# Median and 1x1 mix of a wavelet convolution block: the other term of images 1, 4, 8 and 11 added by TensorE with a unit matrix in place of POOL's five sums

## What is computed

```python
def _L0_conv_ref(x, ...):          # wavelet branches, 3x3 convolution, batch norm with ReLU
    y = lax.conv_general_dilated(rimg, convW_w, window_strides=(1, 1), padding='SAME', ...)
    y = y + convW_b[None, :, None, None]
    return batchnorm_relu(y, bnW_gamma, bnW_beta)

def _L1_conv_ref(x, W, b):
    x_denoised = median_blur(x, KSIZE)                   # 3x3 median of each channel
    y = jnp.einsum('bchw,oc->bohw', x_denoised, W) + b[None, :, None, None]
    return x + y
```

## Time and profile before

| | us |
|---|---|
| median of three runs | 402.18 (400.51, 402.18, 403.07) |
| the profiled execution, its own time | 403.58 |
| its span, first to last instruction | 401.2 |
| busy in the span: PE / PEld / DVE / ACT / POOL | 383.8 / 205.1 / 372.2 / 170.8 / 232.5 |
| mean granted TensorE clock, share of full speed | 0.991 |

### The profile page before, as it was taken

The page is one execution under the profiler, slowest core; times in us unless marked ns, Lnnn a source line. Parts: engine busy times, 40 slices in busy tenths (PEclk is TensorE's granted clock), DMA queues, the critical chain, the costliest instruction groups (busy, mean ns, idle before and its releaser), DMA issues.

```text
span 401.2 us, 3603 instructions
## 1 busy us (share of the span) xinstructions
PE 383.8 (96%) x1106; PEld 205.1 (51%) x1106; DVE 372.2 (93%) x487; ACT 170.8 (43%) x351; POOL 232.5 (58%) x213
## 2 busy tenths in 40 slices
PE   6889999999999999999999999999999999998776
PEld 2245578866454555555555545454545464443222
DVE  2889967999999999999999999999999999999994
ACT  2456674446252433333334343333424221379661
POOL 3999559460694664738474747465564740016791
PEclk9999999999999999999999999999999999999988
DMA  7980010010101001010101010101011000002665
GB/s 290 418 364 2 2 52 2 0 52 2 53 1 52 17 37 52 0 52 0 54 0 52 1 54 1 52 1 52 8 46 33 19 2 1 0 0 119 247 248 223
DMA packets 7793, 26.69 MB, mean 67 GB/s; under 512 B 992, under 2 KB 1248, under 8 KB 7776
## 3 DMA queue, kind: packets, MB, share of 16 engines
q1 hardware_dynamic: 7776, 26.48, 17.6%
HBM read 18.09 MB, written 8.39 MB: 66 GB/s over the span
## 4 chain that ended last, share of the span: by engine, by line
PE 81%; DVE 12%; POOL 3%; DMA 2%; issue 1%; SPq 0%; ACT 0%; DVEq 0%
PE conv_ps L429 60%; PE conv_ps L444 12%; PE one_ps L411 4%; PE one_ps L530 3%; DVE y L1004 2%; PE conv_ps L554 2%; DMA z<-x 2%; POOL y L241 1%; POOL y L242 1%; DVE one_ps L916 1%; DVE one_ps L925 1%; DVE sorted_cols L876 1%; DVE sorted_cols L923 1%; DVE one_ps L910 1%; DVE sorted_cols L883 1%
## 5 line engine op out<-in xcount | busy, mean ns | idle before, releaser
L429 PE MATMUL conv_ps<-ru,wt 128*128 128x512 f32 (+1 forms) x324 | 129.9, 537 | 0.0
L429 PEld LDWEIGHTS conv_ps<-ru,wt 128*128 128x128 f32 x324 | 61.3, 190 | 55.1 <-issue 52.7
L429 PE MATMUL conv_ps<-xu,wt 128*128 128x496 f32 (+3 forms) x216 | 86.6, 537 | 0.0
L663 ACT ACTIVATE y<-conv_ps,sgn 128x512 f32<-128x512 f32 (+1 forms) x36 | 24.4, 679 | 124.1 <-PE conv_ps L429 124.1
L429 PEld LDWEIGHTS conv_ps<-xu,wt 128*128 128x128 f32 x216 | 41.0, 190 | 35.6 <-issue 33.7
L248 POOL TENSOR_TENSOR ru<-z 128x512 f32<-128x512 f32 x14 | 18.2, 1301 | 59.3 <-DVE one_ps L916 59.3
L342 POOL TENSOR_TENSOR ru<-eo 128x512 f32<-128x512 f32 x16 | 17.0, 1062 | 47.5 <-DVE one_ps L874 47.4
L429 PE MATMUL conv_ps<-ru,v 128*128 128x496 f32 (+3 forms) x108 | 43.3, 537 | 0.0
L554 PE MATMUL conv_ps<-z,w 128*128 128x512 f32 x64 | 32.7, 653 | 7.4 <-POOL z L387 4.1
L411 PE MATMUL one_ps<-y,w 128*128 128x512 f32 x64 | 30.5, 601 | 5.1 <-POOL y L242 1.8
L620 ACT ACTIVATE z<-z,bn 128x256 f32<-128x256 f32 x64 | 33.1, 595 | 0.4 <-DVE bn L819 0.4
(11 more groups left out here) (141 smaller groups left out, 741.1 us busy)
## 6 DMA issues: line engine op xcount, KB each, us to landing
z<-x SPq DMA_DIRECT2D x16, 512.0 KB, 10.5
raw_place<-x SPq DMA_DIRECT2D x15, 512.0 KB, 3.2
out<-y SPq DMA_DIRECT2D x15, 512.0 KB, 2.6
wt<-w_t SPq DMA_DIRECT2D x2, 576.0 KB, 10.8
ru<-x SPq DMA_DIRECT2D x1, 512.0 KB, 14.1
out<-y SPq DMA_DIRECT2D x2, 256.0 KB, 2.6
w<-w_t SPq DMA_DIRECT2D x2, 64.0 KB, 7.9
vec<-vectors SPq DMA_DIRECT2D x1, 3.0 KB, 8.3
```

Source lines behind the costliest of these rows:

```text
L429: return nc.tensor.matmul(bank(u, b)[:, (r0 - row) * BW:(r1 - row) * BW], taps(half, kx, ky), plane[:, (r0 + dy) * BW:(r1 + dy) * BW], sta ...
L663: S.activation(at(slot(n), row * W + b, [[2, cols]]), src, ACT.Identity, scale=sgn[:, :], accum_out=y_sum[:, part:part + 1]).then_inc(y_ke ...
```

## The change

Images 1, 4, 8 and 11 (`SUMMED`, four in place of five) get their other term on TensorE. POOL's map makes max(scale3 * y, -shift3) for them, which is ReLU(scale3 * y + shift3) without the shift; behind each of the two products with w2 TensorE multiplies this by a unit matrix into the same bank, so that PSUM holds the sum; ScalarE copies it out to y with the bias shift3 + cb2, and from there it is sent. ScalarE's norm of y (line 720) and POOL's sums (lines 393 and 398) go. The other twelve images are finished as before, by VectorE: images 3, 7, 9 and 12 are new among them, images 4, 8 and 11 have left. The unit matrix is made by POOL (a memset and an affine_select of 128 x 128) in the tensor of w1, which is no longer needed then, once POOL's part in the convolution is done. One column, neg_shift3, is added to the second batch norm. The mix of image 15 goes to `one_ps`, where its own median had its rows, and doesn't wait for image 13 to be read out of `conv_ps`.

```diff
-    SUMMED = (1, 3, 7, 9, 12)
+    SUMMED = (1, 4, 8, 11)
...
+        unit = w1
...
                 if n in SUMMED:
-                    sp.wait_ge(out_by_pool, SUMMED.index(n) + 1)
+                    sp.wait_ge(out_by_act, SUMMED.index(n) + 1)
...
+            G.memset(unit[:, :], 1.0).then_inc(ones_set, 1)
+            pool.wait_ge(ones_set, 1)
+            G.affine_select(out=unit[:, :], in_=unit[:, :], pattern=[[-1, CH]], base=0, channel_multiplier=1,
+                            compare_op=ALU.is_equal, fill=0.0).then_inc(unit_made, 1)
+
             def map_x1(n):
-                G.tensor_scalar(slot(n), slot(n), scale3[:, :], shift3_bias2[:, :], ALU.mult, ALU.add).then_inc(x1_by_pool, 1)
+
+                if n in SUMMED:
+                    G.tensor_scalar(slot(n), slot(n), scale3[:, :], neg_shift3[:, :], ALU.mult, ALU.max).then_inc(x1_by_pool, 1)
+                else:
+                    G.tensor_scalar(slot(n), slot(n), scale3[:, :], shift3_bias2[:, :], ALU.mult, ALU.add).then_inc(x1_by_pool, 1)
...
-                if n in OWN:
-                    map_x1(n)
-                if n - 3 in SUMMED:
-                    pool.wait_ge(x1_by_act, SUMMED.index(n - 3) + 1)
-                    pool.wait_ge(mix_kept, SUMMED.index(n - 3) + 1)
-                    G.tensor_tensor(slot(n - 3), slot(n - 3), zslot(n - 3), ALU.add).then_inc(out_by_pool, 1)
+                map_x1(n)
             map_x1(IMAGES - 1)
...
-            def mix(n, k):
+            def mixed(n):
+
+                return one_ps[:, 0, :] if n == IMAGES - 1 else conv_ps[:, n % 2, :]
+
+            def mix(n):
...
-                    mm = nc.tensor.matmul(conv_ps[:, k, half], w2[:, :], zslot(n)[:, half], start=True, stop=True)
+                    mm = nc.tensor.matmul(mixed(n)[:, half], w2[:, :], zslot(n)[:, half], start=True, stop=n in OWN)
+                    if n in SUMMED:
+                        pe.wait_ge(x1_by_pool, n + 1)
+                        mm = nc.tensor.matmul(mixed(n)[:, half], unit[:, :], slot(n)[:, half], start=False, stop=True)
...
-            for n in range(2, IMAGES):
+            for n in range(2, IMAGES - 1):
                 if n - 2 in SUMMED:
-                    pe.wait_ge(mix_kept, SUMMED.index(n - 2) + 1)
+                    pe.wait_ge(out_by_act, SUMMED.index(n - 2) + 1)
                 else:
                     pe.wait_ge(out_ready, OWN.index(n - 2) + 1)
-                mix(n, n % 2)
+                mix(n)
+            mix(IMAGES - 1)
...
                 norm_median(n)
-                if n in SUMMED:
-                    S.activation(slot(n), slot(n), ACT.Relu, bias=shift3[:, :], scale=scale3[:, :]).then_inc(x1_by_act, 1)
                 if n - 2 in SUMMED:
                     act.wait_ge(mix_done, n - 1)
-                    S.activation(zslot(n - 2), conv_ps[:, n % 2, :], ACT.Identity, bias=cb2).then_inc(mix_kept, 1)
+                    S.activation(slot(n - 2), conv_ps[:, n % 2, :], ACT.Identity, bias=shift3_bias2[:, :]).then_inc(out_by_act, 1)
...
+                after(1)
+                step(V.scalar_tensor_tensor(neg_shift3[:, :], mid3[:, :], scale3[:, :], b3, ALU.mult, ALU.subtract))
                 V.scalar_tensor_tensor(shift3_bias2[:, :], mid3[:, :], neg_scale3[:, :], beta_bias2[:, :], ALU.mult, ALU.add).then_inc(bn3_ready, 1)
...
-                dve.wait_ge(x1_by_pool, OWN.index(n) + 1)
+                dve.wait_ge(x1_by_pool, n + 1)
```

More of the change, by code:

```diff
@@ L124, in wavelet_conv_median_kernel @@
         zero_cols = at(zeros[:, :], 0, [[0, BANK // CH], [1, CH]])
-        singles = sb("singles", [CH, 19])
+        singles = sb("singles", [CH, 20])
         (abs_g3, neg_abs_g3, signed_b, beta_bias2, y_total, sq_total, mean3, off3, neg_off3, sq_eps3, var3, sd3, r3, newton3,
-         scale3, neg_scale3, shift3, shift3_bias2, mid3) = (singles[:, k:k + 1] for k in range(19))
+         scale3, neg_scale3, shift3, shift3_bias2, mid3, neg_shift3) = (singles[:, k:k + 1] for k in range(20))
         conv_ps = ctx.enter_context(nc.psum_tensor("conv_ps", [CH, 2, PIX], fp32))
@@ L189, in wavelet_conv_median_kernel @@
         med_normed = sem("med_normed")
-        x1_by_act = sem("x1_by_act")
         x1_by_pool = sem("x1_by_pool")
@@ L194, in wavelet_conv_median_kernel @@
         mix_done = sem("mix_done")
-        mix_kept = sem("mix_kept")
-        out_by_pool = sem("out_by_pool")
+        ones_set = sem("ones_set")
+        unit_made = sem("unit_made")
+        out_by_act = sem("out_by_act")
         out_ready = sem("out_ready")
@@ L562, in _ @@
             pe.wait_ge(w2_in, 16)
+            pe.wait_ge(unit_made, 1)
             pe.wait_ge(squares_summed, PARTS_ALL)
             for n in range(2):
-                mix(n, n)
-            for n in range(2, IMAGES):
+                mix(n)
+            for n in range(2, IMAGES - 1):
                 if n - 2 in SUMMED:
-                    pe.wait_ge(mix_kept, SUMMED.index(n - 2) + 1)
+                    pe.wait_ge(out_by_act, SUMMED.index(n - 2) + 1)
                 else:
                     pe.wait_ge(out_ready, OWN.index(n - 2) + 1)
-                mix(n, n % 2)
+                mix(n)
+            mix(IMAGES - 1)
         @block.scalar
@@ L997, in second_batch_norm @@
                 step(V.scalar_tensor_tensor(shift3[:, :], mid3[:, :], neg_scale3[:, :], b3, ALU.mult, ALU.add))
+                after(1)
+                step(V.scalar_tensor_tensor(neg_shift3[:, :], mid3[:, :], scale3[:, :], b3, ALU.mult, ALU.subtract))
                 V.scalar_tensor_tensor(shift3_bias2[:, :], mid3[:, :], neg_scale3[:, :], beta_bias2[:, :], ALU.mult, ALU.add).then_inc(bn3_ready, 1)
             def finish(n, first=0, count=PIX, part=0):
-                dve.wait_ge(x1_by_pool, OWN.index(n) + 1)
+                dve.wait_ge(x1_by_pool, n + 1)
                 dve.wait_ge(mix_done, n + 1 + part)
                 v = slot(n)[:, first:first + count]
-                V.scalar_tensor_tensor(v, v, cb2, conv_ps[:, n % 2, first:first + count], ALU.max, ALU.add).then_inc(out_ready, 1)
+                V.scalar_tensor_tensor(v, v, cb2, (one_ps[:, 0, :] if n == IMAGES - 1 else conv_ps[:, n % 2, :])[:, first:first + count], ALU.max, ALU.add).then_inc(out_ready, 1)
             place = {BN3_AT: second_batch_norm}
```

## The result

The changed kernel takes 409.18 us (median of 6 runs, 408.65 to 410.55) against 401.64 us for the kernel before (6 runs, 400.51 to 403.07): ratio 1.0194, 95% interval 1.0168 to 1.0220. It is slower by about 7.5 us. The forecast was 400.0, with 403.2 as the upper end.

A forecast was written before the change was run, and what follows sets the result against it. The last stage was taken as VectorE's until the last median, then TensorE's at half clock. Terms -2.1, +0.13, +1.20 and -1.5 gave -2.3; the schedule's -2.6 was kept, 399.6 by the median, taken as 400.0, range 397.8 to 403.2.

The forecast's parts named there:

- the price of the map: POOL, last stage: each map with a maximum as second operation taken at 1.2 us, bounds 1.2 and 2.4.
- rival D: POOL's maximum map takes 2.4 us: about 0.8 us for four, 400.4; chance 0.46 together with the forecast.
- the new schedule: Last stage, placed instruction by instruction: last median ends at 389.5, last finish at 395.6 instead of 398.2, -2.6 us.
- C: Median run before had full clock at the end, so the change comes out about even: 401.9 us; chance 0.20.
- The unit matrix: Memset and select of 128 columns in POOL's 28.78 us of idle time: taken as 0, select at most 2.4 us.
- The added column of the batch norm: Second batch norm, one column more on VectorE: all the last stage starts 0.13 us later.
- The unit products: TensorE, last stage: eight products at 0.865 us each at full clock, 6.9 us more work.
- The mix of image 15: Put in one_ps at the end of the last stage: worth nothing, since image 13 leaves conv_ps at 392.4, before TensorE's 392.6.
- ScalarE's five norms: Five norms of 1.24 us go from ScalarE: worth nothing by itself, since it waited 5.5 us for mixes anyway.
- A: VectorE stays the bound to the end, with mixes always ready: -4.9 us, 397.3 against the median; chance 0.12.
- B: TensorE's clock falls behind its gap from 375.0: 402.8 us with one fall (chance 0.14), 411 if long (0.08).
- the waits at the end shrink: VectorE's waits for the last mixes fall from 2.52 to 1.05 us, worth -1.5 us.

The follow-up runs named there:

- e1_map_add: Changed kernel with POOL's map of images 1, 4, 8 and 11 as multiply and add, no maximum: 400.34 us, ratio 0.9955 to the kernel before.
- e8: Kernel of e2 with the mix of image 15 back in conv_ps behind the read of image 13: 401.27 us, ratio 0.9994 to e2.
- e2: Changed kernel with the other term of images 1, 4, 8 and 11 made by ScalarE's ReLU, not POOL's map: 401.31 us, ratio 0.9989 to the kernel before.
- e9_forms_long: Kernel before with seven POOL instructions of 1,024 columns on spare data in POOL's idle time: 401.74 us, one run.
- e6: Kernel of e2 with ScalarE's copies out of PSUM one norm later in its order: 400.19 us, ratio 0.9969 to the kernel before.
- e3_forms: Kernel before with eleven POOL instructions, mostly of 512 columns, on spare data in POOL's idle time: 403.99 us, one run.
- e4_no_unit: Changed kernel without the eight unit products, slow map and waits kept: 401.93 us, ratio 1.0006 to the kernel before.
- e7_two_max: Changed kernel with the maximum map for images 1 and 8 only, multiply and add for 4 and 11: 404.38 us, ratio 1.0068 to the kernel before.

## Why the prediction was wrong

**The step that failed** is the price of the map: "four of them with a maximum as the second operation, which no row shows; bounds 1.2 us (the map of rows 6) and 2.4 us (the sum); I take 1.2, since the operands are the same." It takes 3.77 us, outside both bounds. The bounds were taken from rows with the same size and the same or more operands; that assumed that POOL's time goes with columns and operands, not with the operations. The rows could not show otherwise: every tensor_scalar of POOL's in the old trace was multiply-add, the one fast form. The Trainium skill ("GPSIMD Engine Reference", 4.1 Engine selection) calls one-input elementwise work on GpSimd "roughly line-rate"; the runs here agree for multiply-add alone (1.19 us, as long as VectorE's 1.2 for as many columns) and differ for the other forms, which take 2.4 to 3.2 times as long.

**The second step** is rival D, the right rival with a wrong price: "If all sixteen did, the end moves 3.3 us; for four, about 0.8". That counted the slow map as a share of POOL's load. But images of `SUMMED` lie on a ring, and an excess there holds up all engines. The last finish came 8.5 us later than in e1_map_add (403.75 to 395.2). Where the 8.5 us come in, the starts of the first unit product of images 1, 4, 8 and 11 show, in the changed kernel:

```profile
362.48 1.12 PE L563 MATMUL conv_ps<-y,w 128*128 128x512 f32 x2 [2.60 <-POOL y L383]
...
371.57 1.69 PE L563 MATMUL conv_ps<-y,w 128*128 128x512 f32 x2 [1.96 <-POOL y L383]
...
383.96 1.12 PE L563 MATMUL conv_ps<-y,w 128*128 128x512 f32 x2 [0.20 <-POOL y L383]
...
393.05 1.12 PE L563 MATMUL conv_ps<-y,w 128*128 128x512 f32 x2 [1.95 <-POOL y L383]
```

and in e1_map_add:

```profile
359.85 1.12 PE L563 MATMUL conv_ps<-y,w 128*128 128x512 f32 x2
...
367.21 1.02 PE L563 MATMUL conv_ps<-y,w 128*128 128x512 f32 x2
...
377.46 1.02 PE L563 MATMUL conv_ps<-y,w 128*128 128x512 f32 x2
...
384.44 1.02 PE L563 MATMUL conv_ps<-y,w 128*128 128x512 f32 x2
```

The distance grows to 2.6, 4.4, 6.5 and 8.6 us, by 2.6, 1.7, 2.1 and 2.1. In the third step 1.7 are the three products at 1.2 GHz (4.56 us for 2.85), so the map of image 8 itself costs only 0.4. In both kernels TensorE waits 1.38 us for the finish of image 6 before the mix of image 8, and the slow map ends only 0.20 us too late behind that. So the four slow maps cost 6.8 us and the fall of the clock 1.7; four times 2.6, the whole excess each time, would be 10.3. An excess on the ring counts in full only where no other path, here VectorE's, is nearly as long. The waits that close the ring were in the diff and in the order of ScalarE: the products wait for the map, the copy for the products, the norm of the next median stands behind the copy, the corners wait for the norm, and the next map stands behind the corners. I had followed each pair and not the circle.

**What held**, shown by e1_map_add, where only the price of the map is as I had assumed: the new schedule. Its last finish was forecast at 395.6 and came at 395.2. The forecast was 400.0, measured were 400.34. The gain held less well, see C. The unit matrix cost 0.20 and 0.29 us in POOL's idle time. The added column of the batch norm delayed the stage by 0.1. The unit products cost 0.86 us each on the chain, and the last mixes ran without a gap. Line 917 (the old 908) took 1.15 us, 0.43 more than line 914's 0.72, for the map of image 7; line 925 (the old 916) lost nothing. The mix of image 15 was worth nothing (e8). What ScalarE's five norms gave by going wasn't measured by itself; with four of them back, in e2, the time is 1 us longer.

**The rivals.** A didn't come: TensorE had no slack at the end. B, the fall of the clock, did come in the changed kernel, at 372 to 376, behind one of the ring's gaps (1.96 us), and cost 1.7 us; in e1, with one gap of 1.38 us at 375 (1.8 in my schedule), it didn't. The prices given for B don't follow from its own 0.865 us a product: four products are 3.5 us, not 3.2, and no sum is given for the 11.8. C was right on the kernel before. e9_forms_long is that kernel with 0.67 us of delay, and its clock didn't fall at the end, though TensorE has a gap of 1.91 us there as before, then one of 1.47 (1.01 before), and the same 2.09 us of work in a stretch:

```profile
384.00:388.00 4.00, 2.09 (x5) 0.68 (x4) 4.00 (x5) 2.86 (x3) 4.00 (x7) 1.00 0.65 262
388.00:392.00 4.00, 2.53 (x7) 0.90 (x6) 3.97 (x4) 1.12 (x1) 4.00 (x3) 1.00 0.78 316
```

```profile
393.95 2.62 DVE L1026 SCALAR_TENSOR_TENSOR y<-y,vec,conv_ps 128x1024 f32<-128x1024 f32 x3 [0.27 <-PE conv_ps L574]
```

Its last finish ends at 396.6, 395.9 without the delay (C had said 395.5), where the profiled execution of before ended at 398.2. So the fall is worth 2.3 us of that execution, and of the -2.6 us of the forecast most was this: the term "the waits at the end shrink", -1.5, took the half clock of one execution for a cost of the schedule. The prediction says beside it that the clock stands behind this term, but gave C only 0.20.

The timed runs bear this out, since each has its mean granted clock on record. Of the 25 runs of the kernel before beside e1, fourteen have 0.999 or more and take 401.0 us in the median; nine have 0.991, as the profiled execution had, and take 402.0 to 403.9, 402.9 in the median; two lie between, with 0.996. Against the fourteen, e1's 400.34 is 0.65 us less, which is near C's 0 to 0.5; against the median of all, 401.29, it is 0.95 less, where the forecast had 2.2 against the 402.18 of its three runs. So that the forecast's 400.0 fits e1 is in part luck: the median of the three runs lay 0.9 us above that of the 25. The changed kernel has a fall as well, all its six timed runs have a mean clock of 0.995 or less; with the 1.7 us of its profiled execution taken off (an estimate) it would still be 5.8 us behind the kernel before.

## What to carry to other kernels

A row prices an operation with its operators, not only with its size and operands: before work moves to an engine in a new form, the form is timed there, in idle time of the kernel as it is. Where an image goes round several engines that take their work in order, draw the circle that the waits and the orders close; what is added anywhere on it is paid again in every lap, but in full only in laps in which no other path is nearly as long (2.6, 1.7, 0.4 and 2.1 us of 2.6 here), and taking out any one piece helps only until another path is the longer one. A step that closes such a ring (here ScalarE's copy ahead of the next norm) can be moved instead of sped up; e6 got 1.1 us for it. And a row of one profiled execution can hold a fall of the clock that half of the runs don't have: before its waits go into a sum, the mean clocks of the timed runs say how common it is.

## What the runs showed of the hardware

POOL's tensor_scalar on 128 x 1,024 float32 takes 1.19 us for multiply-add, 2.85 for multiply alone or maximum alone, 3.78 for two operations with a maximum or a comparison. By these rows an extra "add zero" would make a multiply faster on POOL; that wasn't tried. A POOL instruction and a VectorE instruction with two SBUF operands hold each other up: such VectorE instructions took 1.60 and 1.76 us instead of 0.70 in e3_forms, and POOL's multiply-maximum 4.82 instead of 3.78 in e9_forms_long. The fall of TensorE's clock to 1.2 GHz isn't decided by one gap alone: behind a gap of 1.91 us the profiled executions of the kernel before and of e3_forms had it in the stretch from 388 to 392 (means of 0.50 and 0.57) and that of e9_forms_long didn't; behind one of 2.6 us at 362 those of e4_no_unit and e7_two_max had it (0.72 and 0.70 from 364 to 368) and that of the changed kernel didn't. What it costs differs too: 2.3 us in the kernel before, where the low clock lasted longer (0.93, 0.50 and 0.72 in three stretches), and about 0.3 in e3_forms (last finish 40.73 us behind the start of the batch norm's last instruction, against 40.47 in e9_forms_long). Why executions differ in this stays open.
